# A decoder layer's first half: an unrolled plan with DMA transposes, and GpSimd multiplying 6 of 16 heads

## The reference

```python
qkv = x @ in_proj_weight.T + in_proj_bias
ac = einsum('tbhd,sbhd->bhts', q + r_w_bias, k)
bd = rel_shift(einsum('tbhd,rhd->bhtr', q + r_r_bias, p))
ctx = einsum('bhts,sbhd->tbhd', softmax((ac + bd) * scale), v)
x = layernorm(x + ctx @ out_proj_weight.T + out_proj_bias)
src_trans = (einsum('bsf,of->bso', ctx_2048, W_src) + b_src) * mask   # keys and values of the second attention
```

## Time and profile before

| | |
|---|---|
| median of 3 runs | 2066.37 us (2063.12 to 2069.61) |
| the profiled execution | 2060.78 us |
| its span, first to last instruction | 2059.0 us |
| PE busy | 1913.1 us, 93% |
| VectorE busy | 1398.1 us, 68% |
| ScalarE busy | 785.1 us, 38% |
| GpSimd busy | 218.0 us, 11% |
| mean granted clock of TensorE | 0.977 |

### The profile page before, as it was taken

The page is one execution under the profiler, slowest core; times in us unless marked ns, Lnnn a source line. Parts: engine busy times, 40 slices in busy tenths (PEclk is TensorE's granted clock), DMA queues, the critical chain, the costliest instruction groups (busy, mean ns, idle before and its releaser), DMA issues. The chain is left out here.

```text
span 2059.0 us, 35403 instructions
## 1 busy us (share of the span) xinstructions
PE 1913.1 (93%) x13100; PEld 1074.0 (52%) x13100; DVE 1398.1 (68%) x1826; ACT 785.1 (38%) x1209; POOL 218.0 (11%) x418
## 2 busy tenths in 40 slices
PE   6999999999999999576899999999999999999998
PEld 5666555555565556333555545445455454554543
DVE  4289978997899889986756565565555655656531
ACT  3422222222212221114846446265363653635522
POOL 0000132012201220230000000100001001010010
PEclk8999999999999999888999999999999999999999
DMA  6112221222122212326531410412304123041010
GB/s 216 37 54 66 83 77 57 73 77 72 62 77 78 67 57 65 115 77 135 178 72 37 98 52 1 103 47 58 92 1 98 52 42 94 16 98 32 1 41 21
DMA packets 151569, 143.10 MB, mean 70 GB/s; under 512 B 55529, under 2 KB 108777, under 8 KB 151426
## 3 DMA queue, kind: packets, MB, share of 16 engines
q1 hardware_dynamic: 147056, 140.58, 24.0%
q10 hardware_dynamic: 4370, 0.34, 0.2%
HBM read 94.75 MB, written 33.55 MB: 62 GB/s over the span
## 5 line engine op out<-in xcount | busy, mean ns | idle before, releaser
L1462 DVE TENSOR_TENSOR p_lo<-k,p_hi 128x1024 f16<-128x1024 f32 x128 | 156.8, 1225 | 192.2 <-ACT p_hi L1350 191.8
L1507 DVE CUSTOM_DVE_ANT_0 junk<-b_sx,mneg 128x512 f16<-128x512 f32 x256 | 175.8, 687 | 31.5 <-issue 22.4
L1151 PE MATMUL b_ff<-x2T_hi,w1T_hi 128*128 128x512 f16 x512 | 194.9, 381 | 2.1 <-DVE x2T_lo L1462 2.1
L1151 PE MATMUL b_ff<-x2T_hi,w1T_lo 128*128 128x512 f16 x512 | 194.8, 380 | 0.0
L1151 PE MATMUL b_ff<-x2T_lo,w1T_hi 128*128 128x512 f16 x512 | 194.8, 380 | 0.0
L1382 ACT ACTIVATE k<-b_st,mbias 128x512 f32<-128x512 f32 x256 | 161.9, 686 | 15.2 <-PE b_st L1195 15.1
L574 PE MATMUL pj_b<-winT_hi,xT_hi 128*128 128x512 f16 x384 | 146.1, 380 | 8.4 <-DVE xT_lo L792 8.4
L1350 ACT ACTIVATE p_hi<-k 128x1024 f16<-128x1024 f32 x128 | 135.3, 1057 | 44.7 <-PE b_av L1210 42.3
L1374 ACT ACTIVATE hq<-b_ff,b 128x512 fp8e4<-128x512 f32 x128 | 88.0, 687 | 155.6 <-PE b_ff L1151 148.9
L574 PE MATMUL pj_b<-winT_lo,xT_hi 128*128 128x512 f16 x384 | 146.0, 380 | 0.0
L574 PE MATMUL pj_b<-winT_hi,xT_lo 128*128 128x512 f16 x384 | 145.9, 380 | 0.0
(11 more groups left out here) (264 smaller groups left out, 4276.7 us busy)
## 6 DMA issues: line engine op xcount, KB each, us to landing
cn<-in_ctx_dram SPq DMA_DIRECT2D x64, 256.0 KB, 2.8
k<-kT_scratch SPq DMA_DIRECT2D x24, 512.0 KB, 7.8
xn<-in_x_dram SPq DMA_DIRECT2D x32, 256.0 KB, 3.0
xres<-in_x_dram SPq DMA_DIRECT2D x32, 256.0 KB, 3.0
x_scratch<-x SPq DMA_DIRECT2D x32, 256.0 KB, 2.0
q<-x_scratch SPq DMA_DIRECT2D x8, 1024.0 KB, 5.7
q<-x_scratch SPq DMA_DIRECT2D x32, 256.0 KB, 4.2
out_dram<-q SPq DMA_DIRECT2D x32, 256.0 KB, 4.3
```

Source lines behind the costliest of these rows:

```text
L1151: mm = pe.matmul(out, a, c, start=(start and n == 0), stop=end)
L1462: dve.tensor_tensor(dst, bank, hi, ALU.subtract).then_inc(out, 1)
L1507: dve.tensor_tensor_reduce(junk[:, :], sx_b[tt % 2][:, :], mneg[:, :], 1.0, NEG, ALU.add, ALU.max, mx[:, h % 2, tt:tt + 1]).then_inc(s["sx ...
```

## The change

The first half no longer has a hardware loop: a class `FirstHalf` lists, for 68 steps (4 blocks of 16, and 4 to finish), which quarters, tiles, transposes and projections belong to each, and every engine writes out its stream from it.

- PE's transposes of x, context and ctx1 are gone. For each tile ("use") ScalarE makes the high half and GpSimd the low half with channels still on the free axis (`row_hi`, `row_lo`, a ring of 3 pairs `rows16`), and SP issues two DMA transposes (`turn`), one for each half, into the same destinations as before. There are 128 uses. PE waits for the DMAs (`wait_turned`).
- GpSimd multiplies heads 10 to 15 of the score products (1536 elements a partition), VectorE heads 0 to 9; VectorE sums both parts in two instructions, GpSimd's part first.
- The three PSUM banks that are set free make rings of 3 for the projections and the quarters, and of 2 for the output projection. The residual is loaded into the tile of its result, with three of them in turn.
- The load stage makes the keys and the first query only; the other queries and `bd` of block 0 come in its score steps. The quarters are spread anew: 10 in block 0, 15 in blocks 1 and 2, 24 in block 3.

```diff
+RING = 3
+POOL_HEADS = 6
+QUARTERS = 8 * NBATCH
+
+
+class FirstHalf:
+
+    STEPS = 16 * NB + 4
+    SCORES_FIRST = (0, 0, 1, 1, 1, 1, 1, 1)
+    SCORES = (1, 1, 2, 1, 2, 1, 2, 1)
+    VALUES = (0, 1, 0, 1, 0, 1, 0, 1)
+    VALUES_LAST = (1, 2, 1, 2, 2, 1, 2, 2)
+
+    def __init__(self):
+        counts = []
+        for b in range(NB):
+            counts += self.SCORES if b else self.SCORES_FIRST
+            counts += self.VALUES if b < NB - 1 else self.VALUES_LAST
+        at, self.by_step = 0, []
+        for n in counts:
+            self.by_step.append(list(range(at, at + n)))
+            at += n
+        assert at == QUARTERS, at
+        self.first_uses = [("x", t) for t in range(T)] + [("c", n) for n in range(5)]
+        order = list(self.first_uses)
+        for g in range(self.STEPS):
+            order += self.uses(g)
+        self.use_no = {use: u for u, use in enumerate(order)}
+        order = [("k", t) for t in range(T)] + [("q", 0)]
+        for g in range(self.STEPS):
+            order += self.projections(g)
+        self.pj_no = {job: n for n, job in enumerate(order)}
+
+    def quarters(self, g):
+
+        return self.by_step[g] if 0 <= g < 16 * NB else []
+
+    def tiles(self, g):
+
+        return [8 * (g // 16) + g % 8] if 0 <= g < 16 * NB and g % 16 >= 8 else []
+
+    def uses(self, g):
+
+        b, t = g // 16, g % 8
+        out = [("o", n) for n in self.tiles(g - 1)]
+        if b < NB - 1 and (1 <= g % 16 <= 8):
+            out.append(("x", 8 * (b + 1) + g % 16 - 1))
+        return out + [("c", n + 5) for n in self.quarters(g) if n + 5 < QUARTERS]
+
+    def turns(self, g):
+
+        late = [use for use in self.uses(g - 1) if use[0] == "c"] if g else [("c", 4)]
+        return late + [use for use in self.uses(g) if use[0] != "c"]
+
+    def loads_after(self, g):
+
+        return [use for use in self.uses(g + 1) if use[0] != "o"]
+
+    def projections(self, g):
+
+        b, t = g // 16, g % 8
+        if g >= 16 * NB:
+            return []
+        if g % 16 < 8:
+            out = [("v", 8 * b + t)]
+            if b == 0:
+                out += [("q", t + 1)] if t + 1 < T else []
+                out.append(("p", t))
+            return out
+        return [(kind, 8 * (b + 1) + t) for kind in "qkp"] if b < NB - 1 else []
+
+
...
-    xres = [sb(f"xres{i}", [P, E], F32) for i in range(2)]
+    rows16 = [pair(f"rows16_{i}", [P, 512]) for i in range(RING)]
-    st_b, xt_b, ct_b = bank("st_b"), bank("xt_b"), bank("ct_b")
-    pj_b = [bank(f"pj_b{i}") for i in range(2)]
-    sm_b = [bank(f"sm_b{i}") for i in range(2)]
-    om_b = bank("om_b")
+    pj_b = [bank(f"pj_b{i}") for i in range(3)]
+    sm_b = [bank(f"sm_b{i}") for i in range(3)]
+    om_b = [bank(f"om_b{i}") for i in range(2)]
...
+            def turn(kind, i):
+
+                u = plan.use_no[kind, i]
+                sp.wait_ge(s["row_lo"], u + 1)
+                if kind == "x" and i >= T:
+                    sp.wait_ge(s["pj_filled"], plan.pj_no["v", i - T] + 1)
+                if kind == "o" and i:
+                    sp.wait_ge(s["om_filled"], i)
+                if kind == "c" and i >= 8:
+                    sp.wait_ge(s["sm_filled"], 4 * (i // 4 - 1))
+                for z in range(2):
+                    sp.dma_start_transpose(turned_into(kind, i, z), rows16[u % RING][z][:, :]).then_inc(
+                        turned[u % RING], 16)
+
...
+            for g in range(plan.STEPS):
+                for n in plan.quarters(g - 1):
+                    store_stage(n)
+                for n in plan.tiles(g - 4):
+                    store_x1(n)
+                for use in plan.turns(g):
+                    turn(*use)
+                for use in plan.loads_after(g):
+                    load_rows(*use)
+                for n in plan.quarters(g):
+                    if n % 4 == 2 and n + 2 < QUARTERS:
+                        load_mask((n + 2) // 4)
+                for n in plan.tiles(g - 1):
+                    load_residual(n)
...
+            def score_products(b, t):
+                if t == 0:
+                    pool.wait_ge(s["pj_copied"], max(plan.pj_no["k", 8 * b + i] for i in range(T)) + 1)
+                    if b:
+                        pool.wait_ge(s["av_done"], 8 * b)
+                else:
+                    pool.wait_ge(s["sc_some"], 8 * b + t)
+                pool.wait_ge(s["pj_copied"], plan.pj_no["q", 8 * b + t] + 1)
+                pool.tensor_tensor(*score_operands(t, by_pool), ALU.mult).then_inc(s["sc_pool"], 1)
+
+            def row_lo(kind, i):
+                u = plan.use_no[kind, i]
+                hi, lo = rows16[u % RING]
+                pool.wait_ge(s["row_hi"], u + 1)
+                pool.tensor_tensor(lo[:, :], row_source(kind, i), hi[:, :], ALU.subtract).then_inc(s["row_lo"], 1)
...
-            def context_transposes(b, off):
-            def x_transposes(b, t):
-            def context1_transposes(b, t):
...
+            def row_hi(kind, i):
+                u = plan.use_no[kind, i]
+                if u >= RING:
+                    act.wait_ge(turned[u % RING], 32 * (u // RING))
+                if kind == "x":
+                    act.wait_ge(xn_ld[i % 2], 16 * (i // 2 + 1))
+                elif kind == "c":
+                    act.wait_ge(cn_ld[i % 2], 16 * (i // 2 + 1))
+                else:
+                    act.wait_ge(s["av_done"], i + 1)
...
-            def context_lo(b, off):
-            def x_lo(b, t):
-            def context1_lo(b, t):
...
                 else:
                     dve.wait_ge(s["sc_done"], 8 * b + t)
-                dve.tensor_tensor(prod[:, :, :], q[:, t, :].unsqueeze(1).to_broadcast([P, T, E]), k[:, :, :],
-                                  ALU.mult).then_inc(s["sc_prod"], 1)
+                dve.wait_ge(s["pj_copied"], plan.pj_no["q", 8 * b + t] + 1)
+                dve.tensor_tensor(*score_operands(t, by_dve), ALU.mult).then_inc(s["sc_prod"], 1)
 
             def score_sums(b, t):
-                dve.wait_ge(s["sc_prod"], 8 * b + t + 1)
-                dve.tensor_reduce(pr[:, t].rearrange("p h s -> p s h"),
-                                  prod[:, :, :].rearrange("p s (h d) -> p s h d", h=H1), AX.X,
-                                  ALU.add).then_inc(s["sc_done"], 1)
+                n = 8 * b + t + 1
+                for heads, ready, done in ((by_pool, "sc_pool", "sc_some"), (by_dve, "sc_prod", "sc_done")):
+                    dve.wait_ge(s[ready], n)
+                    dve.tensor_reduce(pr[:, t].rearrange("p h s -> p s h")[:, :, heads],
+                                      prod[:, :, :].rearrange("p s (h d) -> p s h d", h=H1)[:, :, heads, :], AX.X,
+                                      ALU.add).then_inc(s[done], 1)
 
             def softmax(b):
                 flat = pr[:, :, :, :].rearrange("p t h s -> p (t h) s")
```

More of the change, by code:

```diff
@@ L329, in phase_a @@
[L329 to L336 removed]
+    x1 = [sb(f"x1_{i}", [P, E], F32) for i in range(3)]
@@ L532, in _ @@
+            scale_mask(0)
+            for g in range(plan.STEPS):
+                for n in plan.tiles(g - 3):
+                    norm_factors(n)
+                if g < 16 * NB and g % 16 < 8:
+                    score_products(g // 16, g % 8)
+                for use in plan.uses(g):
+                    row_lo(*use)
+                for n in plan.quarters(g):
+                    if n % 4 == 2 and n + 2 < QUARTERS:
+                        scale_mask((n + 2) // 4)
         @block.tensor
@@ new lines, in output_projection @@
+            def output_projection(n):
+                wait_turned(pe, "o", n)
+                if n >= 2:
+                    pe.wait_ge(s["om_used"], n - 1)
+                out = om_b[n % 2][:, :]
+                for j in range(KT):
+                    for m, (a, c) in enumerate(terms([z[:, j, :] for z in c1T], [z[:, j, :] for z in w.woT])):
+                        pe.matmul(out, a, c, start=(j == 0 and m == 0), stop=False)
+                pe.matmul(out, w.ones[:, 0:P], w.rows[:, BO:BS], start=False, stop=True).then_inc(s["om_filled"], 1)
@@ L603, in context_products @@
+            def context_products(n):
+                c, buf, out = n % 4, (n // 4) % 2, sm_b[n % 3]
+                if n >= 3:
+                    pe.wait_ge(s["sm_lo"], n - 2)
                 if c == 0:
-                    pe.wait_ge(s["st_lo"], n + 4)
-                out = sm_b[off % 2]
+                    for i in range(4):
+                        wait_turned(pe, "c", n + i)
                 if c < 2:
@@ L674, in _ @@
-            av_phase(NB - 1)
-            context1_transposes(NB - 1, 7)
-            output_projection(NB - 1, 7)
+            for g in range(plan.STEPS):
+                for n in plan.tiles(g - 2):
+                    output_projection(n)
+                for n in plan.quarters(g):
+                    context_products(n)
+                for kind, i in plan.projections(g):
+                    projection(kind, i)
         @block.scalar
```

(27 more changed lines are left out.)

600 lines of the change are left out of this document (192 added, 408 removed).

## The result

The changed kernel takes 2014.62 us (median of four runs, 2014.34 to 2015.27) against 2067.99 us for the kernel before on the same chip (2063.12 to 2071.76). The ratio is 0.9744, 95% interval 0.9722 to 0.9766: faster by 53 us. The forecast was 1978, inside its range of 1935 to 2120, and 37 us too low.

The account below looks back on a forecast made before the run. PE bounds the kernel, VectorE nearly as much. Savings of 26 (load stage), 19 (block 0), 48 (blocks 1 and 2) and 11 (block 3), less 16 for late context tiles: net 88, span 1971, median 1978; range 1935 to 2120, likeliest 1935 to 2005.

Parts of the forecast that it names:

- 4 x 8 of waits: Blocks 0 to 3: PE loses 8 us to waits in each, in place of 12.5 before.
- 13 for the tail: End of block 3: high and low halves, transposes, output projection and store after the last result add 13 us.
- late context tiles: Score steps: PE idles 5 us each at quarters 20, 32 and 44, plus 1 for milder ones, 16 us.
- 4 for the slow clock at the start: Load stage: PE's slow clock at the start adds 4 us to a stage of 41 us.
- PE's 56 us: First half: all 128 transpose groups for x, context and ctx1 leave PE, 0.44 us each, 56 us.
- It holds: Turning ctx1 through ScalarE, GpSimd, SP and landing takes 10 to 12 us, within 16 us of room, so no wait.
- Transpose price t = 1.2, landing 2.0: SP's queue: one 128 KB DMA transpose costs 1.2 us, between bounds of 0.4 and 13.8, and lands in 2 us.
- Break-even at t = 2.6: SP's queue: at 2.6 us for one transpose, 68 + 5 + 16 = 89 us are lost, all of the gain.
- rival 2: SP's queue binds above 1.7 us a transpose: 1980 to 2060 in part (0.06), or slower, shared with stalling chains (0.24).
- The split: Score steps: GpSimd's product of 1536 elements takes 3.0 us, at the upper end 3.9; exclusion with VectorE's is covered.
- Rival 1: Score steps: GpSimd or its exclusion with VectorE binds, 48 us back, about 2025; chance 0.12 for 2005 to 2055.
- Block 3, 196 us: Last block of the first half: 174.6 of PE work, 8 of waits, 13 of tail; 196 us, saves 11.

Follow-up runs that it names:

- late output projection: Changed kernel with all heads on VectorE, PE making the output projection after the step's first job: 1989.67 us against 2003.75 without this edit.
- Without the split: Changed kernel with VectorE multiplying all 16 heads, GpSimd keeping only the low halves: 2003.75 us, ratio 0.9707 to the kernel before.
- the stores off SP's queue: Changed kernel with all heads on VectorE, ScalarE issuing the finished quarters' stores in place of SP: 1992.72 us against 2003.75 without this edit.
- twice the load: Changed kernel with an extra 128 KB transpose into an unused tile ahead of each of the 256: 2218.7 us, ratio 1.0745 to the kernel before.
- plain copies: Changed kernel with a plain DMA of the same tile in place of each DMA transpose, values wrong: 1984.71 us, ratio 0.9618 to the kernel before.
- the old loops: Kernel before with only GpSimd multiplying heads 10 to 15 of the score products: 2064.85 us, ratio 0.9997 to the kernel before.
- the best variant: Changed kernel with all heads on VectorE, output projection later and quarter stores on ScalarE's queue: 1977.17 us, ratio 0.9582 to the kernel before.

## Why the prediction was right, and where its sizes were off

The direction, the cause and the place were right: PE lost its transposes, the second half stayed, PE stayed the bound. The forecast's sum was 88 us, and the first half gave 45.5 (936.9 less 891.37). From the windows above, with block 0's first two projections moved to their block, the difference of 43 splits so (the parts add up to 44, since the sum took block 2 as long as block 1):

- **PE's idle time in the blocks: 17 us too little.** Forecast 4 x 8 of waits, 13 for the tail and 16 for late context tiles, together 61, of which 2.8 are PE's own work in the tail; measured 178.87 - 168.05 = 10.8, 16.4, 14.2 and 33.3, together 74.7, and 0.4 ahead of the window.
- **The clock: 25 us, which the sum had at nothing.** PE's work in the blocks was forecast as 172.4 + 178.1 + 178.1 + 174.6 = 703.2 us. Its busy time is 728.3 and the 5.7 in the load stage's window, and 5.6 of it are the two output projections of the tail. "4 for the slow clock at the start" was the only such term. The windows agree roughly: 178.1/0.96 = 185.5 and (174.6 + 5.6)/0.92 = 195.9, against 182.93 to 184.79 and 192.55 measured. The clock's loss isn't new: with the forecast's units, PE's work in the first half was 797 us before and 741 after, an estimate, so 22 us of the old busy time and 28 of the new are slow matmuls. The earlier trace rows had block 3 at 0.91 and its end at 0.84, and the sum took it at full speed.
- **A second output projection in the tail: 3 us.** The sum has one.
- **The load stage: 2 us less than forecast**, 38.8 for 41, and its start 1.4 us later.

Point by point:

- **PE's 56 us.** Right as a count: busy time fell by 51 us, the 56 less some 6 more of slow matmuls.
- **"It holds" (ctx1's chain).** Wrong, and the largest wait: 45 us. The chain was not the error: 9.3 to 9.8 us for the first result of each block, where 10 to 12 was forecast. The room of "a whole step plus VectorE's product, 16" was: PE came for that result between 1.3 us before and 2.8 us after VectorE had finished it. A likely reason is the softmax, which VectorE does ahead of the first values step (9.0 us, from 166.33 to 175.35) and which the forecast's part on VectorE leaves out, while PE goes on with its own work. The queue was a smaller error: "SP 2 to 4" became 8.5 in one stretch (6.0 behind stores and context tiles, then 2.5 of its own), for a wait of 3.5 us. The late output projection, which gives that chain 3 to 5 us more, took 14 us off the time.
- **Late context tiles, 16 us.** Right in kind and in place: quarters 20, 32 and 44, which it named, cost 3.5, 3.5 and 7.8 us, together 14.8 for 15. Two more, 6.5 and 3.7, are at quarters 16 and 28, where a group of four begins as the second quarter of a step. Without the split the 25.0 us are 16.3, and with the stores off SP's queue 10.9.
- **Transpose price t = 1.2, landing 2.0.** 1.20 to 1.27, and 2.4 to 2.5. That the number came out is partly luck: it was worked out for the DMA engines. Their share went from 24.0% of 2059 us to 34.2% of 2013 for 256 transposes, which makes 0.76 us each and 544 packets each, near the 512 of the 256 B case, an estimate that takes the queue's other transfers as unchanged. SP, which no row priced, was the slower one.
- **Break-even at t = 2.6.** Too high. At twice the load the time was 2218.7, where rival 2's formula gives 2048 at t = 2.46 (4.75 x 0.76 x 16 + 1.44 x 8 + 1 = 70 us more than 1978). A straight line through the two measured points (2014.6 at 1.23, 2218.7 at 2.46) crosses the old time at 1.55; the slope below 1.23, from plain copies (30 us for 0.6 us), is flatter and would put it near 2.3. No run lies between; if the cost only steepens with t, the crossing is between the two. The formula took a score step as an average (4.75t), but the queue is in order, and steps with two quarters and a result have six transposes and four stores.
- **The split.** GpSimd's product was put at 3.0 us with 3.9 as its upper end: 3.43 alone, 3.83 on average. The exclusion was right, 2.83 (the mean in the old loops) to 5.70 us on VectorE. Rival 1's cause is therefore real, with a price of 8 to 11 us, not its 48; the forecast had it hidden, and it isn't. The Trainium skill (GPSIMD Engine Reference, Performance versus the Vector engine), by which an element costs about 2.6 cycles there against 1 on VectorE, gave an estimated 3.4 us, and here the trace agrees with its 3.43.
- **Block 3, 196 us.** 225.88. This block got 24 quarters; its values steps have up to six transposes and four stores besides loads, and PE waits there 20.7 us for c1T at a clock of 0.90, after 7.8 for cT in its score steps. Three of the terms above meet in it.

That the best variant's time, 1977 us, equals the forecast is chance: it has neither the split nor the changed kernel's order. The remaining c1T wait there, about 21 us, is the chain from ctx1 to PE, 8.3 to 10.4 us long, which PE meets 2.3 to 8.1 us after VectorE's end; a chain with a shorter low half (up to 4.67 us beside VectorE's products, in place of 1.16) wasn't tried. Why the split costs 8 to 11 us stays open: PE's wait for cT is 9 us longer with it, and VectorE waits 59.1 us for GpSimd's products, but no run separates the two.

## What to carry to other kernels

When a step that one engine did by itself becomes a chain over four engines and a queue, set the end of the producer against the moment at which the consumer comes, for the first item of each phase and not for the average one: here the chain was as long as forecast, and the room for it was missing. Count the queue's issues in the fullest step, and in the order in which they are written. Put work that doesn't need the new tile ahead of the one that does, and move unrelated stores to another queue, before the order of the queue itself is touched. Don't share products over two engines where the bound is a third; and give each stall of PE two prices, its length and the slower matmuls after it.

## What the runs showed of the hardware that wasn't expected

- A DMA transpose of a 128x512 f16 tile from SBUF to SBUF holds SP for 1.20 to 1.27 us, a plain copy of the same tile 0.49 to 0.65 us. Both are above the 0.38 of a store.
- After 3.5 us without a matmul the granted clock was 0.54 for 2.5 us and 0.72 for 2 us; matmuls of 512 columns, 0.22 us apart before (13 in 2.81 us), came 0.43 us apart.
- VectorE's product of 2560 elements that starts behind a GpSimd product takes 5.70 us in place of 2.83, and a GpSimd subtraction of 512 elements beside VectorE's values products 4.67 to 5.21 us in place of 1.16. In the pair shown at 353 us neither was served in part: the later one waited for the whole of the other.
